# Byte pieces widened by ScalarE, and message products two blocks ahead, in a graph network kernel

## What is computed

```python
def step(feat, _):
    transformed = jnp.einsum('nd,khd->knh', feat, W) + b[:, None, :]
    msgs = transformed[etypes, src]
    a = jax.ops.segment_sum(msgs, dst, num_segments=num_nodes)
    feat = _gru_cell(a, feat, w_ih, w_hh, b_ih, b_hh)
    return (feat, None)
feat, _ = jax.lax.scan(step, h, None, length=STEPS)
```

## Time and profile before

| | |
|---|---|
| time, median of 3 runs (lowest, highest) | 7775.96 us (7770.57, 7781.72) |
| profiled execution, own time | 7751.51 us |
| span of that execution | 7749.7 us |
| mean granted TensorE clock | 0.797 |
| busy: PE, PE weight loads, DVE, ACT, POOL | 4891.3, 2487.4, 5101.1, 1287.6, 4049.8 us |
| step 0 | first load 1038 us, end 3103 us |
| ends of steps 1, 2 and 3 | 4104, 5094 and 6053 us |
| moved by DMA | 1414.97 MB |

### The profile page before, as it was taken

How to read it: one execution, slowest core, us unless ns; L and a number is a source line. 1 busy time by engine, 2 the same in 40 slices (tenths; PEclk the granted TensorE clock), 3 DMA queues, 4 the chain that set the end, 5 groups by cost and what they waited for, 6 DMA issues and landing times. The chain is left out here.

```text
span 7749.7 us, 95170 instructions
## 1 busy us (share of the span) xinstructions
PE 4891.3 (63%) x39275; PEld 2487.4 (32%) x39275; DVE 5101.1 (66%) x7708; ACT 1287.6 (17%) x2022; POOL 4049.8 (52%) x3297
## 2 busy tenths in 40 slices
PE   0110157534333334898988998979899647676678
PEld 0110123322112222455544555545555401111123
DVE  9889977534333343676756776657666489999700
ACT  0000012211111110000000000000000157777500
POOL 0027788888888884487872688836883000000130
PEclk9555578767666666999999999989999767667699
DMA  9910046533333337566664666646666143333398
GB/s 413 429 24 0 0 179 255 204 132 140 136 136 128 127 136 150 170 218 206 213 200 151 222 221 204 223 128 235 201 210 216 27 167 150 150 149 152 123 417 363
DMA packets 344776, 1414.97 MB, mean 183 GB/s; under 512 B 129310, under 2 KB 182836, under 8 KB 314516
## 3 DMA queue, kind: packets, MB, share of 16 engines
q1 hardware_dynamic: 159676, 1138.67, 39.3%
q10 hardware_dynamic: 79672, 239.96, 8.7%
q0 software_dynamic: 104992, 30.24, 3.2%
HBM read 1008.21 MB, written 400.36 MB: 182 GB/s over the span
## 5 line engine op out<-in xcount | busy, mean ns | idle before, releaser
L529 PE MATMUL ps_all<-ring,T 128*64 128x448 f16 x32928 | 3318.7, 364 | 1257.4 <-DVE T L1000 1246.7
L529 PEld LDWEIGHTS ps_all<-ring,T 128*64 128x64 bf16 x32928 | 1895.8, 113 | 2662.8 <-DVE T L1000 1280.2
L380 POOL DMA_INDIRECT mat_d<-cT,idxT x1563 | 1966.9, 1258 | 964.9 <-ACT cT L624 488.7
L424 POOL DMA_INDIRECT R<-in_edge_attr,eid x1568 | 1904.7, 1215 | 650.6 <-issue 476.9
L984 DVE TENSOR_SCALAR ring<-ring 128x3136 uint16<-128x3136 uint16 x812 | 803.3, 989 | 1003.3 <-DMA ring<-mat_d 956.1
L985 DVE TENSOR_SCALAR ring<-ring 128x3136 uint16<-128x3136 uint16 x812 | 786.3, 968 | 0.0
L1571 POOL DMA_INDIRECT sg<-seg_d,endI x49 | 57.3, 1170 | 1208.7 <-POOLq L163 1194.0
L483 PE MATMUL ps_all<-ident,R 128*128 128x128 f32 x448 | 108.3, 422 | 810.0 <-DVE R L754 810.0
L678 ACT ACTIVATE R<-R 128x1568 f32<-128x1568 uint16 x196 | 296.1, 1511 | 1749.8 <-DVE R L1021 1519.6
L1514 PE MATMUL ps_all<-ad,ones 3*128 3x384 bf16 (+1 forms) x686 | 321.6, 469 | 342.1 <-ACT ps_all L1484 341.2
L697 ACT ACTIVATE G<-ps_all 64x448 f32<-64x448 f32 x28 | 12.5, 541 | 2855.9 <-PE ps_all L529 2855.9
(11 more groups left out here) (371 smaller groups left out, 3393.5 us busy)
## 6 DMA issues: line engine op xcount, KB each, us to landing
ring<-mat_d SPq DMA_DIRECT2D x784, 784.0 KB
C<-csum_d SPq DMA_DIRECT2D x98, 3136.0 KB, 10.8
mat_d<-ring SPq DMA_DIRECT2D x98, 1568.0 KB, 39.7
csum_d<-R ACTq DMA_DIRECT2D x196, 784.0 KB
seg_d<-R ACTq DMA_DIRECT2D x32, 1568.0 KB, 7.1
msg_d<-t ACTq DMA_DIRECT2D x196, 128.0 KB
R<-in_edge_attr,eid POOLq DMA_INDIRECT x1568
mat_d<-cT,idxT POOLq DMA_INDIRECT x1563
```

What stands on the lines that cost most here:

```text
L380: pool.indirect_dma_start(mat_d, bass.IndirectOffsetOnAxis(idxT[:, col:col + 1], 0), cT[:, col:col + 1], None).then_inc(s_sc[g % 8], 16)
L424: pool.indirect_dma_start(slab[n % 2][:, c, 0:FA], None, attr, bass.IndirectOffsetOnAxis(eid[:, at:at + 1], 0)).then_inc(s_at[n % 2], 16)
L529: mm = pe.matmul(accs[h * D:(h + 1) * D, j, 0:GW], lhsT, ring[:, n % 6, h * HQ + j * GW:h * HQ + (j + 1) * GW], start=first, stop=True, sk ...
```

## The change

Three things. A table made ahead of the build, `WIDENED`, says for each piece which engine widens it and which number the piece has on that engine: ACT all pieces below 196 (the ordinary ones of step 0), above that ACT the odd ones and DVE the even ones. Whoever waited for the semaphore `s_cvd` now waits for the one of the piece's engine. ACT widens with two Copy activations of 3136 bytes each, taken with a step of two bytes, in place of a mask and a shift of 16-bit words. And `T3` and `t32` have three buffers, and PE makes the product of block c+2 during block c, after waiting until DVE has read `psT` (`s_tc`).

ACT's list for block c becomes: widen up to 4c+5, `sums_out(c)`, slab store, `msgs_out(c + 2)`, widen up to 4c+7 (its own pieces each time). DVE's list for block c keeps its order, with `message(c + 2)` for `message(c + 1)`.

```diff
+def widened_by():
+    found, done = [], {"act": 0, "dve": 0}
+    for n in range(STEPS * PPS):
+        who = "act" if n < KT * NB or n % 2 else "dve"
+        done[who] += 1
+        found.append((who, done[who]))
+    return found
+
+
+WIDENED = widened_by()
...
-            T3 = [sb(ph, f"T3{k}", [P, KT, 3 * D], BF16) for k in range(2)]
+            T3 = [sb(ph, f"T3{k}", [P, KT, 3 * D], BF16) for k in range(3)]
...
-            t32 = sb(ph, "t32", [P, 2, KT * D])
+            t32 = sb(ph, "t32", [P, 3, KT * D])
...
+            def widened(eng, n):
+                who, nth = WIDENED[n]
+                eng.wait_ge(s_cva if who == "act" else s_cvd, nth)
+
+            def widen_ready(eng, n):
+                eng.wait_ge(s_ld[n % 4], 16 * (n // 4 + 1))
+                if n >= 6:
+                    eng.wait_ge(s_us, n - 5)
...
                             if n >= 4:
-                                sp.wait_ge(s_cvd, n - 3)
+                                widened(sp, n - 4)
...
-                        pe.wait_ge(s_cvd, n + 1)
+                        widened(pe, n)
...
-                                if i == 44 and c + 1 < NB:
-                                    product(st, c + 1)
+                                if i == 44 and c + 2 < NB:
+                                    pe.wait_ge(s_tc, NB * st + c + 2)
+                                    product(st, c + 2)
...
                     product(st, 0)
+                    pe.wait_ge(s_tc, NB * st + 1)
+                    product(st, 1)
...
+                        if WIDENED[n][0] == "act":
+                            widen_ready(act, n)
+                            two, to = (z.rearrange("p (t n) -> p t n", t=2) if k else z.rearrange("p (n t) -> p t n", t=2)
+                                       for k, z in enumerate((raw[:, n % 4, :], ring[:, n % 6, :].bitcast(U16))))
+                            act.activation(to[:, 0, :], two[:, 0, :], ACT.Copy)
+                            act.activation(to[:, 1, :], two[:, 1, :], ACT.Copy).then_inc(s_cva, 1)
...
                 for st in range(STEPS):
+                    upto(piece_no(st, 0, 0))
                     msgs_out(st, 0)
+                    upto(piece_no(st, 0, KT - 1))
+                    msgs_out(st, 1)
                     for c in range(NB):
+                        upto(piece_no(st, c, 0) + 5)
                         if st == 0:
                             sums_out(c)
                         at = slab_of(st, c)
                         if at is not None and at[1] == 3:
                             stored(at[0])
-                        if c + 1 < NB:
-                            msgs_out(st, c + 1)
+                        if c + 2 < NB:
+                            msgs_out(st, c + 2)
+                        upto(piece_no(st, c, 0) + 7)
+                    upto(PPS * (st + 1) - 1)
                     grown(st)
...
-                        dve.wait_ge(s_ld[n % 4], 16 * (n // 4 + 1))
-                        if n >= 6:
-                            dve.wait_ge(s_us, n - 5)
-                        two, to = raw[:, n % 4, :].bitcast(U16), ring[:, n % 6, :].bitcast(U16)
-                        dve.tensor_scalar(to[:, 0:HQ], two, 255, None, ALU.bitwise_and)
-                        dve.tensor_scalar(to[:, HQ:NP], two, 8, None, ALU.logical_shift_right).then_inc(s_cvd, 1)
+                        if WIDENED[n][0] == "dve":
+                            widen_ready(dve, n)
+                            two, to = raw[:, n % 4, :].bitcast(U16), ring[:, n % 6, :].bitcast(U16)
+                            dve.tensor_scalar(to[:, 0:HQ], two, 255, None, ALU.bitwise_and)
+                            dve.tensor_scalar(to[:, HQ:NP], two, 8, None, ALU.logical_shift_right).then_inc(s_cvd, 1)
...
                     message(st, 0)
                     upto(piece_no(st, 0, KT - 1))
+                    message(st, 1)
...
-                        if c + 1 < NB:
-                            message(st, c + 1)
-                        else:
+                        if c + 2 < NB:
+                            message(st, c + 2)
+                        elif c + 1 == NB:
                             message_extra(st)
```

More of the change, by code:

```diff
@@ L264, in build @@
                 "extratable", "extrarows")))
-            (s_cvd, s_us, s_T, s_tm, s_tc, s_csm, s_cse, s_csr, s_te, s_m3) = sems(ph, *(t + n for n in (
-                "converted", "pieceused", "msgs", "products", "productsread", "summed", "sumsb", "sumread", "extramsgs", "extraparts")))
-            s_td = sems(ph, t + "msgsout0", t + "msgsout1")
+            (s_cva, s_cvd, s_us, s_T, s_tm, s_tc, s_csm, s_cse, s_csr, s_te, s_m3) = sems(ph, *(t + n for n in (
+                "widenedact", "wideneddve", "pieceused", "msgs", "products", "productsread", "summed", "sumsb", "sumread", "extramsgs", "extraparts")))
+            s_td = sems(ph, *(t + f"msgsout{k}" for k in range(3)))
             s_cso = sems(ph, t + "sumout0", t + "sumout1")
@@ L394, in gathered @@
                     n = NB * (st + 1)
-                    pool.wait_ge(s_td[0], 16 * ((n + 1) // 2))
-                    pool.wait_ge(s_td[1], 16 * (n // 2))
+                    for k in range(3):
+                        pool.wait_ge(s_td[k], 16 * ((n + 2 - k) // 3))
                     for g in range(NX):
@@ L666, in msgs_out, with upto @@
                     act.dma_start(msg_d[c * P * KT:(c + 1) * P * KT, :].rearrange("(p k) d -> p (k d)", k=KT),
-                                  t32[:, b % 2, :]).then_inc(s_td[b % 2], 16)
+                                  t32[:, b % 3, :]).then_inc(s_td[b % 3], 16)
+                converted = 0
+                def upto(last):
+                    nonlocal converted
+                    while converted <= last:
+                        n = converted
+                        if WIDENED[n][0] == "act":
[4 more added lines that the diff above has]
+                            act.activation(to[:, 1, :], two[:, 1, :], ACT.Copy).then_inc(s_cva, 1)
+                        converted += 1
                 def sums_out(c):
@@ L989, in message @@
                     b = NB * st + c
-                    to, own = T3[b % 2], t32[:, b % 2, :]
+                    to, own = T3[b % 3], t32[:, b % 3, :]
                     r3, t3 = (z.rearrange("p (k m) -> p k m", k=KT) for z in (r32, own))
                     dve.wait_ge(s_tm, b + 1)
-                    if b >= 2:
-                        dve.wait_ge(s_td[b % 2], 16 * (b // 2))
+                    if b >= 3:
+                        dve.wait_ge(s_td[b % 3], 16 * (b // 3))
                     dve.tensor_tensor(own, psT, biasB[:, :], ALU.add).then_inc(s_tc, 1)
@@ L1015, in added @@
                     four = [ring[:, piece_no(0, c, k) % 6, :].bitcast(U16) for k in range(KT)]
-                    dve.wait_ge(s_cvd, piece_no(0, c, KT - 1) + 1)
+                    widened(dve, piece_no(0, c, KT - 1))
                     if c:
```

2 lines of the change are left out of this document (1 added, 1 removed).

## The result

The kernel after takes 7566.0 us (median) against 7773.3 us of the kernel before on the same chip: a ratio of 0.9738 [0.9713, 0.9763], faster by about 205 us. Forecast were 7543 us and a range of 7480 to 7680: the sign and the range hold, the time is 23 us above the forecast. The profiled execution took 7588.8 us, the longest of the three that count.

What follows compares the result with a forecast made beforehand. GpSimd's issue of indirect DMAs was taken to set the pace of step 0 and most of steps 1 to 3. -110 + 8 - 126 - 5 = -233 us gave 7518.5, plus 24.5 carried over 7543 us; range 7480 to 7680.

Steps and rivals of the forecast that it cites:

- Step 0, widening off DVE: Step 0's scatter on GpSimd: freed from DVE's widening, it gains 2.3 us for each of 48 blocks, 110 us.
- ACT in step 0: ACT's widening in step 0: 2.82 us a half piece, 35 us a block, meeting the scatter near block 30 to 40.
- the first rival: ACT becomes step 0's bound: mild form 7590 us, chance 0.12; full form, alternating with additions, 8085 us, chance 0.07.
- The end of step 0: Stretch after the last scatter: ACT's late last pieces cost +8 us, bounds -5 to +25, mostly covered by the late T3e.
- the additions keep their 6.9 us: Step 0: three scatters per block meet DVE additions and lose 3 x 2.3 us, which the change leaves in place.
- Steps 1 to 3, every other piece: Slab gathers on GpSimd: halving DVE's widening gains 4.5 us a slab (2.5 to 6), 126 us over 28 slabs.
- The second rival: Steps 1 to 3: halving DVE's widening doesn't relieve the gathers, only step 0 gains; 7669 us, chance 0.12.
- the third: Rival: ScalarE's widening holds GpSimd up as much as DVE's, leaving only -5 and +8; 7779 us, chance 0.06.
- wait of 73 us for a slab store: Steps 1 to 3: GpSimd waits for a slab store once a step, at the start, 73 us.
- The sign at DVE: Sign of being right: DVE's waits for the edge gather get shorter by about a third.
- ACT in steps 1 to 3: ACT's widening in the later steps costs 0; if its cover went, 3.7 us at each of 28 slabs.
- Messages two ahead: PE gains about a quarter block, 4 us, once per step during a slab stall; counts only in step 3, -5 us.

Runs made afterwards that it cites:

- e0: The kernel after, with only a bounds check added to SyncE's reads of the group counts (as in all follow-up runs); 7578.5 us, ratio 0.9744 to before.
- e1: The kernel after, but ACT widens in step 0 alone and DVE widens every piece of steps 1 to 3; 7668.1 us, ratio 0.9855 to before.
- e2: The kernel after, but DVE widens all of step 0 and ACT only every other piece in steps 1 to 3; 7656.3 us, ratio 0.9842 to before.
- e3: The kernel after, but DVE widens everything, leaving only the messages two blocks ahead; 7750.6 us, ratio 0.9958 to before.
- e6: The kernel before, with the unused places of the ext_d writes 512 bytes apart instead of in adjacent bytes; 7702.9 us, ratio 0.9915 to before.
- e5: The kernel after, with the unused places of the ext_d writes 512 bytes apart instead of in adjacent bytes; 7514.3 us, ratio 0.9666 to before.
- e10: The kernel after, with two of the three additions summing a block's pieces in step 0 left out (results differ); 7390.1 us, ratio 0.9486 to before.
- e7: The kernel after, with DVE widening the last four blocks of step 0 and unused ext_d places 512 bytes apart; 7488.8 us, ratio 0.9632 to before.
- e8: e7, but in steps 1 to 3 DVE widens pieces 0 and 1 of each block, ACT 2 and 3; 7518.2 us, ratio 0.9659 to before.
- e9: e7, but in steps 1 to 3 ACT widens two of every three pieces instead of one of two; 7458.2 us, ratio 0.9584 to before.

## Why the prediction was right, and where it was off

The sum was -110 + 8 - 126 - 5 = -233. Term by term, by the profiled executions of before against after (and e0):

| term | predicted | after | e0 |
|---|---|---|---|
| scatter of step 0 | -110 | -100 | -114 |
| end of step 0 | +8 | +50 | +50 |
| steps 1 to 3 | -131 | -112 | -109 |
| rest | 0 | -1 | -1 |

These make -163 for after where -233 were predicted, 70 us apart. The forecast is only 23 us from the median, because 47 us lie between the executions: the profiled one of before took 24.5 us less than the median it was given, and I carried that over; the profiled one of after took 22.8 us more than its median. Where in the kernel these 47 us lie can't be told. So that the time came out this near is in part luck.

*Step 0, widening off DVE*: right in mechanism and size. The price of 2.3 us a block, inferred from the pattern of single scatters, gave 110; 100 to 118 were measured (before against after, and against e1). Single differences of this column can be off by 26 us; the four executions with DVE on step 0 (before, e2, e3, e6) average 2964.6 us and the four with ACT on it (after, e0, e1, e5) 2848.3, which is 116, and the delays of the scatters themselves fall by 111 us. The choice behind it, that the additions keep their 6.9 us, was right as well (e10).

*ACT in step 0*: 2.81 us against 2.82. In the catch-up its widening of a block starts every 33.4 us (1064.8 to 1933.0, 26 blocks) where I took 35, and from block 27 on every 43 to 52 us, when it waits for the scatter; I had put the meeting near block 30 to 40. So the first rival, ACT as the bound at 37.3 us a block, did not come, and the fall to slower from 42 us was far. The sign that I named for it, ACT busy without idle time at 2500 us, is absent: in 1480 to 2850 us it is busy for 928 of 1370.

*The end of step 0*: here the step failed. I took +8 us with bounds of -5 and +25, "nearer to the low end because T3e is late anyway and covers most of it"; +50 came. T3e covers little, since it moved itself: in DVE's list it stands behind the additions of block 48, these need ACT's last piece of that block, and T3e came 50 us later behind the last scatter (113.7 to 163.5 us), with 31 us from there to the step's end before and after. All the cover there was is the 12.2 us that T3e waited for the messages before. The price of the queue was too low as well: it was made of single pieces at 5.6 against 2 us. ACT took 33 us for a block with its row counts, so it was behind when the scatter ended: in the kernel before blocks 46 and 47 were widened 20 us apart (2916.0 and 2935.9 us), in e5 35.6 us apart (2825.3 and 2860.9), and block 48 was done 79 us after the last scatter where DVE needs 27 (e5, e7). That is 42 of the 50 us (e5 to e7). The rest, some 10 us, comes only beside the adjacent bytes, where ACT stands 69.3 us before a write of `sums_out`. In the kernel before ACT waited at most 9.5 us for such a write in this stretch; the crawl fell on the loads of block 48, for which DVE waited 75.6 us, and so most of it was in the step's time already. That transfers crawl for 70 us and that the widening stands in ACT's queue were both known when the +8 was set.

*Steps 1 to 3, every other piece*: 4.5 us a slab were predicted (2.5 to 6), 3.2, 4.2 and 3.5 us came (before to after); of this the widening gives 2.9 us (e3 to e0), and the rest, 0.6 us with the messages, is within the spread. So the size lay near the low bound, which was the bound of "single pieces meet relatively more gathers". e8 speaks against that reason, as pairs are no better than singles; e9, in which the remaining pieces cost more than the first, was not foreseen by either. The second rival (no relief) and the third (ACT holds GpSimd as DVE does) are excluded by e2 and by the 0.96 us. The prediction's wait of 73 us for a slab store, once a step, holds for step 1 alone: in the kernel before it is 154 us in step 2 and 155 in step 3, and 152 and 158 after, so it didn't bear on the sum.

*The sign at DVE*: I expected its waits for the gather to shrink by a third. They did not, though the slab got shorter: that wait measures the difference of two lists that both moved.

*ACT in steps 1 to 3* at cost 0: one sign of being wrong did come, PE waits 40.2 us for its pieces in step 1's slabs. But its wait of 64.8 us for T is gone from the list, and the slabs are still GpSimd's (575.4 + 149.1 = 724.5 of 736 us).

*Messages two ahead* were priced at -5, in step 3 only; they gave 32 us [22 to 44], so this term failed in size. I took one stall per step of 4 us. In the profiled executions steps 1 to 3 are 28 us shorter in e3, 10 of them at the end of step 3, and the gathers together take 17 us less, which I did not look for. The mechanism isn't shown.

*End of step 3* at 5820 us: 5892 came, which is the 70 us of the sum.

## What to carry to other kernels

When work moves into another engine's queue, follow what then stands behind it in every list, not only in that queue: what is "late anyway" covers a delay only if it doesn't itself wait for the delayed work. Here it did, by way of the additions in DVE's list, and the cover was 12 us where most of the delay was expected to vanish. An engine that is not the limit may still be slowed through its neighbour, and the way to price that is one instruction's duration beside and not beside the other; here 0.5 us a scatter gave 110 us, and 111 to 116 were measured. When a part of an engine's work is cheap to have elsewhere only in the mean, give it back where the arrivals bunch: four blocks of 49 were worth 25 us.

## What the runs showed of the hardware beyond that

- **One-byte writes to adjacent addresses in DRAM crawl, and hold others up.** Eight indirect DMAs of 128 bytes landed in 54.9 us; with the unused places 512 bytes apart in 5.8 us. The 784 KB row counts beside them went from 39.1 to 10.0 us (after against e7). It was worth 58 us of tail in the kernel before (e6, ratio 0.9915), with not one byte less moved (1414.97 MB in both). Whether the adjacency or the common 512 bytes matters, and whether a smaller step would do, was not tried.
- **An addition of two SBUF inputs of 16 bits holds up the indirect DMAs that GpSimd issues**, by about 2 us for one of 3.43 us (e10); a scatter beside one takes 3.15 to 3.31 us instead of 0.96.
- **ScalarE reads bytes with a stride of two at no extra price**: 3136 elements a partition in 2.80 to 2.82 us, the 2.82 us of its float activation of the same size.
